# Turning the operands of the experts' up products round: weights stationary, merged rows in a bank of their own

## The reference, cut to what matters

```python
def _moe(x, topk_idx, topk_w, w1, w2, w3):      # E 32 experts, K 4 of them for a token, CAP 128 slots, H 512, F 256
    ...
    h = silu(einsum('ech,ehf->ecf', buf, w1)) * einsum('ech,ehf->ecf', buf, w3)
    ob = einsum('ecf,efh->ech', h, w2)
    y = ob[flat_e, slot]                        # every slot's result is weighted by topk_w and added to its token's row
    return (y.reshape(n, K, H) * topk_w[:, :, None]).sum(1)
```

## Time and profile before

| | |
|---|---|
| median of three runs | 1617.62 us |
| the profiled execution | 1617.22 us |
| its span, first to last instruction | 1615.1 us |
| TensorE busy | 1599.7 us, 99% of the span |
| VectorE, ScalarE, GpSimd busy | 1221.8, 844.5, 796.6 us |
| granted TensorE clock | 1.000 on average |

### The profile page before, as it was taken

The page is one execution under the profiler, slowest core; times in us unless marked ns, Lnnn a source line. Parts: engine busy times, 40 slices in busy tenths (PEclk is TensorE's granted clock), DMA queues, the critical chain, the costliest instruction groups (busy, mean ns, idle before and its releaser), DMA issues. The chain is left out here.

```text
span 1615.1 us, 33871 instructions
## 1 busy us (share of the span) xinstructions
PE 1599.7 (99%) x11431; PEld 1074.5 (67%) x11431; DVE 1221.8 (76%) x3524; ACT 844.5 (52%) x2086; POOL 796.6 (49%) x1092
## 2 busy tenths in 40 slices
PE   8999999999999999999999999999999999999998
PEld 5666666666666666666666666666767766666664
DVE  7988787878787787878787877878767256776775
ACT  6764544554545545445545455454534156666664
POOL 3444646464554646464645546464445542433332
PEclk9999999999999999999999999999999999999999
DMA  8765555354544554444545444554457568988855
GB/s 255 188 156 118 106 93 110 76 113 85 120 88 117 101 117 104 94 111 88 114 100 117 89 116 101 117 104 90 97 150 255 125 196 222 273 235 223 248 117 99
DMA packets 400235, 219.26 MB, mean 136 GB/s; under 512 B 348464, under 2 KB 356656, under 8 KB 400064
## 3 DMA queue, kind: packets, MB, share of 16 engines
q1 hardware_dynamic: 384176, 191.80, 47.6%
q0 software_dynamic: 15328, 24.25, 8.8%
q10 hardware_dynamic: 560, 1.05, 0.2%
HBM read 92.92 MB, written 40.80 MB: 83 GB/s over the span
## 5 line engine op out<-in xcount | busy, mean ns | idle before, releaser
L982 ACT ACTIVATE arena<-arena,neg_max 128x256 f32<-128x256 f32 x512 | 253.7, 496 | 378.5 <-DVE neg_max L1291 378.5
L727 POOL TENSOR_SCALAR arena<-arena,prob_scale 128x256 f16<-128x256 f32 x384 | 186.8, 503 | 470.1 <-DVE prob_scale L1300 468.0
L1671 PE MATMUL ps_query<-xn_both,arena 128*128 128x256 f16 x1024 | 279.1, 273 | 1.0 <-DMA xn_both<-xn_half 1.0
L1672 PE MATMUL ps_query<-xn_both,arena 128*128 128x256 f16 x1024 | 279.1, 273 | 0.0
L1673 PE MATMUL ps_query<-xn_both,arena 128*128 128x256 f16 x1024 | 279.1, 273 | 0.0
L1308 DVE SCALAR_TENSOR_TENSOR arena<-arena,prob_scale 128x256 f16<-128x256 f32 x384 | 239.5, 672 | 9.3 <-POOL arena L727 9.1
L1291 DVE CUSTOM_DVE_ANT_0 arena<-ps_score,mask_add 128x256 f32<-128x256 f32 x512 | 186.3, 420 | 79.0 <-PE ps_score L1673 79.0
L1671 PE MATMUL ps_out<-arena,o_t 128*128 128x512 f16 x512 | 194.1, 379 | 0.7 <-DVE o_t L1313 0.6
L1672 PE MATMUL ps_out<-arena,o_t 128*128 128x512 f16 x512 | 194.0, 379 | 0.0
L1673 PE MATMUL ps_out<-arena,o_t 128*128 128x512 f16 x512 | 194.0, 379 | 0.0
L777 POOL DMA_INDIRECT slot_table<-entry,slot_at x128 | 130.3, 1018 | 48.0 <-issue 33.8
(11 more groups left out here) (345 smaller groups left out, 3958.8 us busy)
## 6 DMA issues: line engine op xcount, KB each, us to landing
arena<-w SPq DMA_DIRECT2D x96, 512.0 KB, 6.4
x_in<-x SPq DMA_DIRECT2D x15, 512.0 KB, 3.8
out_rows_dram<-x SPq DMA_DIRECT2D x30, 256.0 KB, 2.4
xn_rows<-xn_half SPq DMA_DIRECT2D x15, 512.0 KB, 3.1
out_rows_dram<-weight_in POOLq DMA_DIRECT2D x28, 256.0 KB, 5.7
x2t_kept<-xn_both SPq DMA_DIRECT2D x12, 512.0 KB, 3.0
ctx_in<-ctx_t SPq DMA_DIRECT2D x16, 256.0 KB, 3.1
weight_in<-wq SPq DMA_DIRECT2D x8, 512.0 KB, 5.2
```

The source lines that it names most:

```text
L727: pool.tensor_scalar(p_rows[:, 0, c, :], probs[:, c, :], prob_scale[:, c:c + 1], 1.0, ALU.mult, ALU.mult).then_inc(norm_hi, 1)
L982: act.activation(probs[:, c, :], probs[:, c, :], ACT.Exp, bias=neg_max[:, c:c + 1], scale=-1.0, accum_out=prob_sum[:, c:c + 1]).then_inc(e ...
L1671: pe.matmul(dst, a.hi, b.hi, start=start and n == 0, stop=False)
L1672: pe.matmul(dst, a.hi, b.lo, start=False, stop=False)
```

## The change

The operands of `expert_up` change places: blocks of 128x128 of the weights become stationary, and the rows stream past as 128 columns. 48 matmuls of 128 columns take the place of 12 of 512. The result then has inner values on partitions and slots along the columns, so nothing has to be turned; `expert_ht_high` and `expert_ht_low` read `expert_h` in SBUF. The block of weights is every second column (`c f` with f inner), so that the inner values match the rows of w2 as before.

The routing weight is no longer a scalar of a partition of `expert_h`; it moves behind the down product, into the scale of `scale_y`, `pair_high` and `pair_rest`. A merged row has the odd expert's weight, so it can't be added in the even expert's bank: `merge` writes `ps_head`, and VectorE adds that to the even expert's scaled y by a new instruction, `join_y`. `add_rows` of an even expert waits for it. Of `expert_hidden` the transpose of the token numbers is left, once per pair (`spread_rows`); it waits until `ps_head` has been read by `join_y`.

```diff
@@ -233,6 +233,7 @@
         slot_weight = sbuf("slot_weight", [E])
+        pair_weight = sbuf("pair_weight", [E])
         expert_tanh_g = k_both[:, :, :].rearrange("p h s -> p (h s)").bitcast(F32)
@@ -472,9 +474,9 @@
-        def scaled_at(e):
-            return e if e % 2 else e + 2
+        def y_ready(e):
+            return (scaled_y if e % 2 else joined_y), e // 2 + 1
@@ -787,7 +789,7 @@
             def add_rows(e):
-                pool.wait_ge(scaled_y, scaled_at(e))
+                pool.wait_ge(*y_ready(e))
                 pool.wait_ge(added, adds_before["x", e])
@@ -1021,29 +1023,31 @@
             def expert_ht_high(e):
-                act.wait_ge(pe_eht, e + 1)
+                act.wait_ge(ehid, e + 1)
                 if e >= 2:
                     act.wait_ge(pe_ey, e - 1)
-                act.activation(expert_h_t[e % 2].hi, ps_head[:, 0:FB * P].rearrange("p (f c) -> p f c", f=FB), ACT.Copy,
-                               scale=1.0).then_inc(eht_hi, 1)
+                act.activation(expert_h_t[e % 2].hi, expert_h, ACT.Copy, scale=1.0).then_inc(eht_hi, 1)
...
                 else:
-                    act.wait_ge(pe_merged, e // 2 + 1)
+                    act.wait_ge(pe_ey, e + 1)
                 if e >= 6:
...
                     act.wait_ge(out_xn2, 16 * B)
-                act.activation(expert_y[e % 6], y_bank(e)[:, :], ACT.Copy, scale=1.0 / EY_S).then_inc(scaled_y, 1)
+                act.activation(expert_y[e % 6], y_bank(e)[:, :], ACT.Copy, scale=slot_weight[:, e:e + 1]).then_inc(
+                    scaled_y if e % 2 else own_y, 1)
...
                     act.wait_ge(pe_merged, e // 2)
-                act.activation(pair_y.hi, y_bank(e)[:, :], ACT.Copy, scale=PAIR_S / EY_S).then_inc(pair_hi, 1)
+                else:
+                    act.wait_ge(table_scaled, 4)
+                act.activation(pair_y.hi, y_bank(e)[:, :], ACT.Copy, scale=pair_weight[:, e:e + 1]).then_inc(pair_hi, 1)
@@ -1119,7 +1123,7 @@
                     expert_tanh(e)
-                if e >= 3 and e % 2:
+                if 3 <= e < E and e % 2:
                     scale_y(e - 3)
@@ -1139,6 +1143,8 @@
                     scale_y(e - 1)
+                if e == E:
+                    scale_y(e - 2)
                 if e in BESIDE:
@@ -1439,24 +1445,25 @@
                 if e:
-                    dve.wait_ge(pe_eht, e)
-                dve.scalar_tensor_tensor(expert_h, gated[:, :], slot_weight[:, e:e + 1], ps[:, F:2 * F], ALU.mult,
+                    dve.wait_ge(eht_hi, e)
+                    dve.wait_ge(eht_lo, e)
+                dve.scalar_tensor_tensor(expert_h, gated[:, :], 0.5 * GLU * GLU * HE_S, ps[:, F:2 * F], ALU.mult,
                                          ALU.mult).then_inc(ehid, 1)
...
                 dve.wait_ge(eht_hi, e + 1)
-                dve.scalar_tensor_tensor(expert_h_t[e % 2].lo, ps_head[:, 0:FB * P].rearrange("p (f c) -> p f c", f=FB),
-                                         1.0, expert_h_t[e % 2].hi, ALU.mult, ALU.subtract).then_inc(eht_lo, 1)
+                dve.scalar_tensor_tensor(expert_h_t[e % 2].lo, expert_h, 1.0, expert_h_t[e % 2].hi, ALU.mult,
+                                         ALU.subtract).then_inc(eht_lo, 1)
...
                 m = e // 2
-                dve.wait_ge(pe_eht, e + 2)
+                dve.wait_ge(pe_spread, m + 1)
                 dve.wait_ge(table_scaled, 3)
...
                     dve.wait_ge(pe_merged, m - 1)
-                dve.tensor_scalar(pair_match[m % 2], ps_head[:, FB * P:(FB + 1) * P], row_f[:, e + 1:e + 2], EY_S / PAIR_S,
-                                  ALU.is_equal, ALU.mult).then_inc(*own.up())
+                dve.tensor_scalar(pair_match[m % 2], ps_head[:, 0:P], row_f[:, e + 1:e + 2], 1.0 / PAIR_S, ALU.is_equal,
+                                  ALU.mult).then_inc(*own.up())
                 dve.wait_ge(*own.now())
@@ -1465,8 +1472,13 @@
                 dve.wait_ge(pair_hi, e // 2 + 1)
-                dve.scalar_tensor_tensor(pair_y.lo, y_bank(e + 1)[:, :], PAIR_S / EY_S, pair_y.hi, ALU.mult,
+                dve.scalar_tensor_tensor(pair_y.lo, y_bank(e + 1)[:, :], pair_weight[:, e + 1:e + 2], pair_y.hi, ALU.mult,
                                          ALU.subtract).then_inc(pair_lo, 1)
+            def join_y(e):
+                dve.wait_ge(own_y, e // 2 + 1)
+                dve.wait_ge(pe_merged, e // 2 + 1)
+                dve.tensor_tensor(expert_y[e % 6], ps_head[:, :], expert_y[e % 6], ALU.add).then_inc(joined_y, 1)
@@ -1622,17 +1634,20 @@
...
+            dve.tensor_scalar(pair_weight[:, :], slot_weight[:, :], PAIR_S, None, ALU.mult).then_inc(table_scaled, 1)
             for k in range(21, EARLY):
                 piece(k)
-            for e in range(E + 1):
+            for e in range(E + 2):
                 if e < E:
                     expert_glu(e)
+                if e >= 3 and e % 2:
+                    join_y(e - 3)
                 if e >= 1 and e - 1 + HELD < E:
@@ -1835,30 +1845,27 @@
                 pe.wait_ge(rows_copied, e + 1)
-                for part in range(2):
-                    pe.wait_ge(expert_lo[part], e + 1)
                 if e < 2:
...
                     pe.wait_ge(ehid, e - 1)
-                w = Split(*(half[:, 0:2 * THIRD].rearrange("p (m k n) -> p k m n", m=2, k=KD)
-                            for half in (expert_w[e % HELD].hi, expert_w[e % HELD].lo)))
-                products(ps_score[e % 2][:, :].rearrange("p (m n) -> p m n", m=2),
-                         [(rows_t[e % 2][:, k, :], w[:, k]) for k in range(KD)]).then_inc(pe_eup, 1)
-            def expert_hidden(e):
-                pe.wait_ge(ehid, e + 1)
+                for part in range(2):
+                    pe.wait_ge(expert_lo[part], e + 1)
+                    w = Split(*(half[:, part * THIRD:(part + 1) * THIRD].rearrange("p (k c f) -> p k f c", k=KD, f=FB)
+                                for half in (expert_w[e % HELD].hi, expert_w[e % HELD].lo)))
+                    for f in range(FB):
+                        n = (part * FB + f) * P
+                        m = products(ps_score[e % 2][:, n:n + P], [(w[:, k, f, :], rows_t[e % 2][:, k, :])
+                                                                   for k in range(KD)])
+                m.then_inc(pe_eup, 1)
+            def spread_rows(e):
+                pe.wait_ge(table_scaled, 3)
                 if e:
-                    pe.wait_ge(eht_lo, e)
-                    pe.wait_ge(matched, e // 2)
+                    pe.wait_ge(joined_y, e // 2)
                 else:
                     pe.wait_ge(head_lo, TURNS)
-                cols = expert_h.rearrange("c (p f) -> c f p", f=FB)
-                columns = [cols[:, f, :] for f in range(FB)]
-                if e % 2:
-                    pe.wait_ge(table_scaled, 3)
-                    columns.append(row_f[:, e - 1:e].broadcast_to([P, P]))
-                transposes(ps_head, columns, pe_eht)
+                pe.transpose(ps_head[:, 0:P], row_f[:, e:e + 1].broadcast_to([P, P]), ident[:, :]).then_inc(pe_spread, 1)
@@ -1866,20 +1873,20 @@
                 elif e % 2:
-                    pe.wait_ge(scaled_y, scaled_at(e - 2))
+                    pe.wait_ge(*y_ready(e - 2))
                 elif e == 2:
...
                 else:
-                    pe.wait_ge(scaled_y, scaled_at(e - 4))
+                    pe.wait_ge(own_y, e // 2 - 1)
                 w = expert_w[e % HELD][:, 2 * THIRD:]
                 products(y_bank(e)[:, :], [(expert_h_t[e % 2][:, f, :], w[:, f * D:(f + 1) * D])
-                                               for f in range(FB)], stop=e % 2 == 1).then_inc(pe_ey, 1)
+                                           for f in range(FB)]).then_inc(pe_ey, 1)
...
                 pe.wait_ge(pair_lo, e // 2 + 1)
-                pe.matmul(y_bank(e)[:, :], pair_match[e // 2 % 2], pair_y.hi, start=False, stop=False)
-                pe.matmul(y_bank(e)[:, :], pair_match[e // 2 % 2], pair_y.lo, start=False, stop=True).then_inc(pe_merged, 1)
+                pe.matmul(ps_head[:, :], pair_match[e // 2 % 2], pair_y.hi, start=True, stop=False)
+                pe.matmul(ps_head[:, :], pair_match[e // 2 % 2], pair_y.lo, start=False, stop=True).then_inc(pe_merged, 1)
@@ -1949,8 +1956,8 @@
                     expert_rows(e + 2)
-                if e < E:
-                    expert_hidden(e)
+                if e < E and e % 2:
+                    spread_rows(e - 1)
                 if e in BESIDE:
```

More of the change, by code:

```diff
@@ L42 @@
 GLU = 1.0 / (W_S * X_S)
-EY_S = HE_S * W_S / ROUTE_SCALE
+EY_S = HE_S * W_S
 PAIR_S = 16.0
@@ L316, in build @@
             signal(n) for n in ("pe_x2t", "pe_gate", "pe_rank", "pe_up", "pe_down"))
-        pe_rows, pe_eup, pe_eht, pe_ey = (signal(n) for n in ("pe_rows", "pe_eup", "pe_eht", "pe_ey"))
+        pe_rows, pe_eup, pe_spread, pe_ey = (signal(n) for n in ("pe_rows", "pe_eup", "pe_spread", "pe_ey"))
```

(18 more changed lines are left out.)

## The result

Eight runs of the changed kernel have a median of 1613.57 us (1612.62 to 1614.07), eight of the kernel before, on the same chip, 1618.20. The ratio is 0.9972, with a 95% interval of 0.9961 to 0.9982: faster by 0.28%, some 4.6 us. The forecast was 1613.1 us, 4.5 us less than before. The profiled execution has a span of 1611.5 us; that of before had 1615.1.

The account below looks back on a forecast made before the run. TensorE was taken to bound the stage by issue alone. Turning -7.7, up products +2.7 and the stretch without pieces +0.5 gave -4.5 us: 1612.7 from the profiled 1617.22, plus 0.40 for the median, 1613.1; range 1611.0 to 1617.0.

Parts of the forecast that it names:

- The bound: Beside the pieces TensorE bounds the stage by issue alone: a matmul removed or added is worth its distance to the next.
- The up product: In each expert, 48 matmuls at 0.056 us take 2.69 us instead of 2.59: +0.10 us, +2.7 over 27 iterations.
- The rival of exposed loads: Weight loads in the up products don't stay hidden; fully exposed at 113 ns, 87 us slower than forecast; chance 0.08.
- the 81 ns of the Trainium skill: Rule for streamed loads and 128-column matmuls: an up product takes 3.89 us, the kernel 1651.5; chance 3%.
- The turning: Transposing hidden values on TensorE disappears, leaving one float32 transpose in odd iterations at 0.13 us: -7.7 us together.
- The cover beside the pieces: VectorE's added join fits its idle time, slack 0.25 and 0.38 us, so pieces aren't delayed: counted as nothing.
- The rival of VectorE's lateness: The join delays reading the first piece by up to 0.3 us in 13 iterations: 4 us return, 1617 us; chance 0.12.
- Behind the pieces: In the stretch without pieces, joins on nearly full VectorE delay what TensorE needs: +0.5 us, ends -1.5 and +1.4.
- The scales of the y copies: On VectorE and ScalarE, scales become columns instead of numbers: counted as nothing, 0.06 us each without idle time.
- The wait of 1 to 2 us at the merge of pair 26: After the pieces, TensorE's merge for experts 26 and 27 waits because VectorE comes 0.65 us later, TensorE some 1.0 sooner.
- The third rival: The chain of adds at the end sets the time alone and can lose 1 to 2 us: 1615 us; chance 0.05.
- Two ends of the range: Limits tied to the stretch without pieces, -1.5 or +1.4 in place of +0.5; own range 1611.0 to 1614.4 us.

Follow-up runs that it names:

- join_column: The changed kernel with `join_y` adding only one column of 512: 1610.62 us, ratio 0.9971 against the kernel before.

## Why the prediction was right

- **The bound.** It said that TensorE bounds the stage by issue alone, so each matmul is worth its distance. The up products and the turning taken apart add up to the whole within 0.01 us: shown. The stage was forecast 5.0 us shorter and is 5.06; a part of that closeness is luck, because the up products cost 0.3 us less than forecast (2.44 for 2.7) and the turning gave 0.2 less (7.49 for 7.7).
- **The up product** was put at +0.10 us by eight matmuls in a row, and measured +0.09 over 48 in a row. The rival of exposed loads is refuted by 55.8 ns here, and by 29 for 64 columns. The trace disagrees as well with the 81 ns of the Trainium skill ("TensorE: Matmul & The Clock Gate", section "Back-to-back issue gap"), which gave 1651.5 us.
- **The turning.** The 0.29 us went in full; the single transpose cost 0.11, not 0.13. The 0.11 us of waiting at expert 0 was replaced by a wait in its iteration, for a piece's bank, which I hadn't seen: the piece starts 0.40 us behind the turned rows, listed as a wait of 0.24, so that iteration gained nothing from its turning. Of the 0.40, 0.11 were lost before too, which leaves 0.3. In sum 27 x 0.09 - 14 x 0.29 - 13 x 0.29 + 0.3 = -5.1 us; -5.0 was forecast and -5.06 measured. A pair of experts takes 0.39 us less (19.81 for 20.20), where 0.36 was said.
- **The cover beside the pieces** held: no waits from expert 1 on. The join itself takes 0.685 us, for the 0.69 forecast. The rival of VectorE's lateness is refuted for the join as it is, but doubling it brought 1.70 us in the stage, at four of the odd iterations. So the slack was less than one more join in these only.
- **Behind the pieces** +0.5 us was forecast, and +0.7 and +0.6 measured in two profiles of the changed kernel; the spread of the end is as large as the term, so that this agrees in size shows little. The adds tell more. The down product of expert 29 was forecast 0.7 us later and its scaled copy 0.6; they came 0.88 and 0.89 later, and the add 0.98. The join is the largest part: without it the add of expert 29 comes 0.90 us sooner, with two of them 1.45 later. The rest balances. The turning left out alone brings this add forward by 0.45 us, the new up products alone move it back by 0.09 (23.62), and join_column has it at 23.61, which is 0.44 us later than these two leave it.
- **The scales of the y copies**, counted at nothing with 0.06 us as an end, cost 0.09 us on ScalarE and 0.06 on VectorE. Where VectorE and ScalarE idle this is covered, as said. Three of these instructions stand between the down product of expert 29 and its add, 0.24 us in a row, yet from the start of the first to the add it is only 0.10 us more (3.61 for 3.51). Others stand ahead of that. How much of the 0.44 us is theirs, and how much the move of `scale_y` or what is left of the join, wasn't tried alone.
- **One step went another way than told.** The wait of 1 to 2 us at the merge of pair 26 was forecast and came (1.2 us), but put down partly to the join. It is as long with the turning alone left out (1.4 us) and with the join on one column (1.2): the join makes VectorE late by 0.53 us here, but TensorE too, through its wait at the spread.
- **The third rival**, that the adds hold the end, is refuted: counted from the up product of expert 0, the last add starts 4.21 us sooner than before (300.30 for 304.51), and with the turning alone left out the kernel gained 7.8 us. The 0.2 us forecast between the last two adds came (1.85 us apart, 2.10 before).
- **Two ends of the range** don't follow from their terms: 1613.1 with -1.5 in place of +0.5 is 1611.1, not 1611.0, and with +1.4 it is 1614.0, not 1614.4. The measured 1613.57 lies inside either way.

## What to carry to other kernels

Which operand is loaded is nearly free on TensorE as long as the columns stay the same in number: 48 loads and matmuls of 128 columns cost some 3.5% more than 12 of 512 (2.68 and 2.59 us), and a turning that the other choice spares is a clear gain where TensorE is dense. A step that leaves TensorE for a vector engine needs a look at every stretch by itself: the join was free where VectorE idles for a quarter of the time, and cost 0.9 us on the way to the adds where VectorE has little idle time. There, moving waits about changed their place, and their sum hardly or for the worse.

## What the runs showed of the hardware

A ScalarE copy with a scale from a column of SBUF takes longer than one with a number. The first line is the kernel before, by line and shape (busy us, mean ns, idle):

```profile
L1046 ACT ACTIVATE o_t<-ps_out 128x512 f16<-128x512 f32 x16 | 9.6, 598 | 13.9 <-PE ps_out L1673 13.9
```

and the changed kernel:

```profile
L1050 ACT ACTIVATE o_t<-ps_out,pair_weight 128x512 f16<-128x512 f32 x16 | 11.0, 688 | 14.0 <-PE ps_out L1688 14.0
L1041 ACT ACTIVATE x<-ps_out,slot_weight 128x512 f32<-128x512 f32 x9 | 6.2, 683 | 0.8 <-DMA out_rows_dram<-xn_both,table 0.8
```

On VectorE the same change of a scalar costs 0.06 us, for 256 columns (L1450 against the 481 ns of L1443 in the earlier trace rows) as for 512, L1475 against L1468 of the kernel before (the last line, 1343 to 1444 us):

```profile
L1450 DVE SCALAR_TENSOR_TENSOR mask_add<-gated,ps_score 128x256 f32<-128x256 f32 x32 | 13.5, 421 | 1.1
L1475 DVE SCALAR_TENSOR_TENSOR o_t<-ps_out,pair_weight,o_t 128x512 f16<-128x512 f32 x16 | 11.9, 745 | 1.2 <-ACT o_t L1050 1.2
L1468 DVE SCALAR_TENSOR_TENSOR o_t<-ps_out,o_t 128x512 f16<-128x512 f32 x5 | 3.4, 682 | 0.0
```

A load of 128x128 float16 values takes 98 ns for columns side by side and two apart, and 113 in the turning of the gathered rows, whose columns are four apart; whether the distance or the turning makes that difference wasn't tried. And loads keep up with a matmul every 29 ns, a third of the time that one load is listed with.
